# Key transposes at three due times, and block 0's second mixing, low-rank store and weight sums at other quarters, in an attention and FFN kernel

## The reference

```python
h = einsum('bct,bcd->bdt', x, W[condition])          # mixes the 64 rows of a batch
q, k, v = h @ Wq.T, h @ Wk.T, h @ Wv.T               # 32 heads, 8 key/value heads, 128 wide
q, k = rmsnorm(q), rmsnorm(k)
x = x + softmax(q k^T / sqrt(128) + alibi) v @ Wo.T
x = x + FFN(low_rank_adapted_linear(x))              # FFN weights: base plus a Fourier update
```

## Time and profile before

| | |
|---|---|
| median of 3 runs | 2388.41 us (2387.01 to 2389.78) |
| the profiled execution | 2391.09 us, of which 2389.2 us is the span from the first to the last instruction |
| TensorE busy | 2349.9 us of the span, 98% |
| VectorE, ScalarE, GpSimd busy | 1775.3, 1468.2, 284.6 us |
| TensorE clock | full, but for one stretch of about 13 us near 153 us, and the last microseconds |
| DMA | 316.16 MB, 132 GB/s over the span |

### The profile page before, as it was taken

The page is one execution under the profiler, slowest core; times in us unless marked ns, Lnnn a source line. Parts: engine busy times, 40 slices in busy tenths (PEclk is TensorE's granted clock), DMA queues, the critical chain, the costliest instruction groups (busy, mean ns, idle before and its releaser), DMA issues.

```text
span 2389.2 us, 33429 instructions
## 1 busy us (share of the span) xinstructions
PE 2349.9 (98%) x11706; PEld 1964.7 (82%) x11706; DVE 1775.3 (74%) x2930; ACT 1468.2 (61%) x3625; POOL 284.6 (12%) x336
## 2 busy tenths in 40 slices
PE   8989999999999999999999999999999999999998
PEld 6878888888888888888888888888888888888886
DVE  6768868696847878787846777777866686969691
ACT  4246667576625857576824857576844676767660
POOL 1222010101011001010021101010121101010111
PEclk9989999999999999999999999999999999999999
DMA  6765434442542242424443242423254242424250
GB/s 256 261 240 209 156 133 151 148 138 69 196 147 88 86 143 73 144 76 133 138 155 115 71 159 71 159 71 124 93 174 141 81 150 71 147 83 137 69 201 35
DMA packets 88440, 316.16 MB, mean 132 GB/s; under 512 B 12716, under 2 KB 13228, under 8 KB 87124
## 3 DMA queue, kind: packets, MB, share of 16 engines
q1 hardware_dynamic: 70292, 247.14, 31.3%
q0 software_dynamic: 16256, 62.92, 7.3%
q10 hardware_dynamic: 1728, 3.98, 0.5%
HBM read 282.54 MB, written 31.46 MB: 131 GB/s over the span
## 4 chain that ended last, share of the span: by engine, by line
PE 86%; DVE 8%; DMA 2%; issue 2%; ACT 1%; POOL 0%; ACTq 0%; DVEq 0%; POOLq 0%
PE main L1027 73%; PE qt_bank L1188 3%; PE s_bank L1204 3%; DVE ring L1497 2%; PE s_bank L1205 2%; PE pv_bank L1225 1%; PE pv_bank L1224 1%; PE pt_bank L1212 1%; PE pt_bank L1027 1%; DVE values L1628 1%; DVE lefts L1497 1%; DMA sums<-in_wo 1%; DVE quads L1715 1%; DMA acc<-in_x 1%; DVE qn L1642 1%
## 5 line engine op out<-in xcount | busy, mean ns | idle before, releaser
L1027 PE MATMUL main<-ring,act_hi 128*128 128x512 f32 x3584 | 1149.4, 402 | 1.1 <-DVE ring L1497 0.6
L1027 PEld LDWEIGHTS main<-ring,act_hi 128*128 128x128 f32 x3584 | 642.6, 189 | 114.8 <-issue 3.0
L1027 PE MATMUL main<-ring,act_lo 128*128 128x512 f32 x1792 | 702.7, 392 | 0.0
L1027 PE MATMUL main<-ring,lefts 128*128 128x512 f32 x2688 | 626.2, 392 | 0.0
L1497 DVE TENSOR_TENSOR ring<-raw,ring 128x1024 fp32r<-128x1024 f32 x448 | 548.3, 1229 | 51.0 <-ACT ring L1235 49.4
L1027 PEld LDWEIGHTS main<-ring,lefts 128*128 128x128 f32 x2688 | 500.2, 188 | 101.3
L1235 ACT ACTIVATE ring<-raw 128x1024 fp32r<-128x1024 f32 x448 | 472.3, 1057 | 174.7 <-PE main L1027 158.2
L1027 PEld LDWEIGHTS main<-ring,act_lo 128*128 128x128 f32 x1792 | 337.4, 188 | 74.5
L1836 POOL TENSOR_TENSOR rstd<-mean,half 128x4 f32<-128x4 f32 (+1 forms) x192 | 173.8, 905 | 1559.9 <-DVE mean L1622 1555.0
L1368 ACT ACTIVATE sq<-main 128x128 f32<-128x128 f32 x640 | 168.6, 276 | 78.1 <-PE main L1027 72.9
L1396 ACT ACTIVATE prob<-score,peak 128x64 f32<-128x64 f32 x512 | 136.1, 336 | 97.0 <-DVE peak L1680 96.3
(11 more groups left out here) (168 smaller groups left out, 2571.8 us busy)
## 6 DMA issues: line engine op xcount, KB each, us to landing
raw<-in_wq SPq DMA_DIRECT2D x128, 512.0 KB, 4.3
raw<-t_scratch SPq DMA_DIRECT2D x128, 512.0 KB, 3.3
raw<-in_wo SPq DMA_DIRECT2D x96, 512.0 KB, 3.3
raw<-in_wkv SPq DMA_DIRECT2D x64, 512.0 KB, 4.0
sums<-in_wo POOLq DMA_DIRECT2D x32, 512.0 KB, 8.0
t_scratch<-sums POOLq DMA_DIRECT2D x32, 512.0 KB, 4.1
raw<-f_scratch SPq DMA_DIRECT2D x32, 512.0 KB, 5.2
acc<-in_x POOLq DMA_DIRECT2D x16, 512.0 KB, 4.2
```

The source lines that it names most:

```text
L1027: mm = eng.matmul(bank, a, b, start=start and n == 0 and m == 0, stop=stop and n == len(terms) - 1 and m == 2, skip_group_check=further)
```

## The change

The due times of `key_t`, `k_hi` and `k_lo` are no longer one for all: for kv0 of blocks 1 to 3, the first three steps have 2.8, 3.4, 3.9 ("mixing"); the last step of kv1, kv2 and kv3 of each block has 4.8, 5.4, 5.9 ("projection": the `o` unit follows it); all others keep 3.8, 4.4, 4.9 ("queries"). In block 0 the mixing of tiles 2 and 3 goes from quarters 5 and 9 to 2 and 6, `fx_store` from quarter 4 to 14, the t1 to t4 and stores of the first round in `blocks()` by 3.5 quarters later (its loads stay), and the next two rounds, loads and all, by 1.5 quarters later.

```diff
-          tq=2.8, tq_hi=3.4, tq_lo=3.9, tk=3.8, tk_hi=4.4, tk_lo=4.9,
+          tq=2.8, tq_hi=3.4, tq_lo=3.9,
...
+KEYS_AT = dict(mixing=(2.8, 3.4, 3.9), queries=(3.8, 4.4, 4.9), projection=(4.8, 5.4, 5.9))
...
+FIRST_MIX = 2, 2
...
-ROUND_AT = (0.5, 17, 33.5, 104, 180)
+ROUND_AT = (0.5, 18.5, 35, 104, 180)
...
-        self.at(0, 4, lambda: self.add("fx_store"))
+        self.at(0, 14, lambda: self.add("fx_store"))
...
+            wait = 3.5 if start < QUARTERS else 0
             for i, stage in enumerate(("t1", "t2", "t3", "t4")):
-                self.at(start, 7.2 + 1.5 * i, lambda pair=pair, c=c, stage=stage: self.sums_add(pair, c, [stage]))
-            self.at(start, 12.8, lambda pair=pair, c=c: self.sums_store(pair, c))
+                self.at(start, wait + 7.2 + 1.5 * i, lambda pair=pair, c=c, stage=stage: self.sums_add(pair, c, [stage]))
+            self.at(start, wait + 12.8, lambda pair=pair, c=c: self.sums_store(pair, c))
...
-            if k in (1, 2):
-                self.later(1, lambda k=k: self.mix(0, k + 1))
+            if k in (0, 1):
+                self.later(FIRST_MIX[k], lambda k=k: self.mix(0, k + 2))
...
+        (kind, blk, n), i = self.units[self.steps[k][0]], self.steps[k][1]
+        if n == 0:
+            place = "mixing" if blk > 0 and i < TILES - 1 else "queries"
+        else:
+            place = "projection" if i == TILES - 1 else "queries"
+        transposed, upper, lower = KEYS_AT[place]
...
-            self.at(base, AT["tk"], transpose)
+            self.at(base, transposed, transpose)
...
-            self.at(base, AT["tk_hi"], lambda: self.add("k_hi", k))
-            self.at(base, AT["tk_lo"], lambda: self.add("k_lo", k))
+            self.at(base, upper, lambda: self.add("k_hi", k))
+            self.at(base, lower, lambda: self.add("k_lo", k))
```

## The result

The changed kernel takes 2373.85 us in the median of 5 runs (2372.03 to 2375.95), the kernel before 2387.01 beside it (5 runs, 2384.35 to 2389.78): ratio 0.9943, 95% interval 0.9932 to 0.9953, 13.2 us or 0.55% faster. The forecast was 2367.0 with 2362 to 2377 as its range: the direction and the range held, and of the 21.5 us expected only about 13 came. The time lies outside the 2362 to 2371 of the forecast's own case, in the 2372 to 2377 of rival B. The profiled execution took 2375.95 us (span 2374.0), 15.1 less than the 2391.09 of before. Lines of the kernel are 14 higher now: L1041 is the main matmul, L1202 the transposes, L1125 and L1127 the mixing, L1656 the scale, L1663 the gain.

What follows compares the result with a forecast made beforehand. TensorE, busy 98% of the span, bounds the kernel by its work plus its holes. Gains of 11.5 (projection), 0.9 (mixing) and 9.1 (block 0) sum to 21.5 us: 2388.41 less that is 2366.9, forecast 2367, range 2362 to 2377.

Steps and rivals of the forecast that it cites:

- the forecast's own case: Whole kernel: all three gains come, 21.5 us together, for 2362 to 2371 us; chance 0.74.
- rival B: Block 0: POOL gives the start back, late store landings delaying loads and the first query's `rstd`; 2372 to 2377, chance 0.15.
- Projection, 12 x 0.96 = 11.5 us: Last step of kv1 to kv3: key transposes a quarter later no longer wait for `gain`, 0.96 us each, twelve times.
- Rivals C and E: `o` unit: C, projection waits only move, 2378.5, chance 0.05; E, `k_hi` makes ring halves late, 2394, chance 0.03.
- Block 0, 9.1 us: Start of block 0: 10.5 us gained by the second key transpose, less 0.9 and 0.5 given back.
- I take 0.5: Block 0, first queries: POOL's `rstd` blocked by the second round's loads, between 0 and 5.5 us, taken as 0.5.
- The loss at the start: Block 0, first quarter to second key transpose: 32.47 us holding 20.06 us of work at full clock, so 12.4 lost.
- The sums of rounds 2 and 3 ... taken as 0: Block 0: these sums each move one place on, with the same DVE work, +/-1 us, taken as 0.
- Mixing, 0.9 us: Block transitions: `k_lo` empties `qt_bank` sooner for the last mixing, 0.43 us back at two of three transitions.

Runs made afterwards that it cites:

- e4: The changed kernel with `fx_store` at quarter 8 in place of 14: 2376.64 us, ratio 0.9961 to the kernel before.
- e6: The changed kernel with the second round's four loads 2.9 quarters later, behind the first query's `rstd`: 2371.62 us, ratio 0.9932; a second time 2370.59 us, 0.9924.
- e8: The changed kernel with the second round's loads behind the first query's `rstd` and all keys at the places of before: 2384.78 us, ratio 0.9982.

## Why the prediction was right, and where it was not

- **Projection, 12 x 0.96 = 11.5 us: right.** The stretches gave 11.3, the kernel with this part alone 11.3 in its medians (9.8 by its ratio, 6.7 to 13.1 by its interval). Rivals C and E are out: no wait moved into the `o` units. The kernel with block 0 mended shows the other side, the twelve waits of 8.8 us with the keys where they were.
- **Block 0, 9.1 us: wrong, it was 0.** The step that failed is "I take 0.5, ... since before the change the last load came 6.2 us after the stores' issue ... and the same distance here gives a load at about 173.5". It came at 177.67, 9.6 us after the stores' issue ended: the last store took 9.8 us to land in place of 6.4. The same distance could not be carried over, since other transfers now run beside the stores. Without `fx_store` beside them the last store took 8.4 us in place of 9.8 (e4). That the DMA engines no longer stand idle ahead of the stores is not it either: in the kernel with the store at 8 they moved 0 GB/s from 161 to 166 us, and the stores took up to 8.4. What all nine profiles with the changed block 0 share is the raw-weight load issued 0.9 us behind the first t store and the next 2.3 us later; in the three with the old one, the first comes 5.0 to 5.3 us behind it. This sorts the profiles, last store 8.4 to 11.1 us against 6.4, but no run moves the raw loads alone, so it is argued and not shown. The hole and the clock behind it cost 6.8 us in B, and 5.9 in the block-0 kernel. I had written down the rival with this mechanism and gave it 0.15; its cause, `fx_store`, explains less than half of the lateness (e4), its queue the right one (e6). That the range held is this rival's doing: the sum itself was 6.9 us off.
- **The loss at the start was overrated.** 12.4 us were read from one profile. With the same code in block 0, A was 1.8 and 3.9 us shorter in two others; against the mean of the three (42.2) A gained 7.3, where the profiled pair shows 9.05. The chain of steps in A was right to 0.6 us; what it was subtracted from was an execution with an unusually large loss.
- **"The sums of rounds 2 and 3 ... taken as 0": 1.2 us** in C, in all four kernels. The two profiles show where: a score wait of 0.66 at 232.6 that before had not, and 0.79 in place of 0.57 and 0.67 at two query transposes.
- **Mixing, 0.9 us: the size per case was right, the sum can't be measured.** Each case is a transition at which TensorE waits for `k_lo`. From the start of `x_hi` to the mixing it is 725.91 - 722.75 = 3.16 us before, and 2.71 in the changed kernel, ScalarE's and TensorE's timelines at block 2's transition:

```profile
1272.33 1.06 ACT L1249 ACTIVATE x_odd<-acc 128x1024 fp32r<-128x1024 f32 x1 [3.34 <-DMA acc<-in_x]
...
1275.04 0.39 PE L1125 MATMUL qt_bank<-mixw,x_odd 128*128 128x256 f32 x1 [0.66 <-DVE k_t L1511]
```

  0.45 us, forecast 0.43. The other profiles agree: the distance is 3.15 us at each of the five such waits in kernels with the old places (before, projection alone, e8) and 2.7 us at each of the eight in kernels with the new ones. But how large the hole is, and at how many of the three transitions there is one (none to two), differs between executions: in the changed kernel run again the same hole is 1.76, and the transition 52.15 us against 49.95. The 2.6 us by which the profiled pair differs here are mostly chance: in the projection and block-0 kernels, with the key places of before, all six transitions had 48.5 to 49.9 us too. By the runs the part is 0.9996 [0.9987, 1.0005], which can't be told from nothing.
- **Together:** by the experiments 11.3 + 0 + some 0.9 = 12.2, measured 13.2 (11.2 to 16.2 by the interval) and, the second time, 9.9 (7.4 to 13.9). The best version is the changed kernel with the four loads behind the `rstd`: 16.5 and 19.2 us faster than before in the medians of its two measurements.

## What to carry to other kernels

Where an engine's queue holds both computations and DMA issues that wait for landings, note for each such issue when it leaves the queue and when the next computation behind it is wanted: that margin (here 4.6 us) is what an earlier start uses up if the landings don't come earlier with it, as here, where the stores were issued 4.3 us earlier and the last load left at the same time. A hole with a half-clock stretch behind it should be read from several executions before its length is booked as a gain. And a transpose that waits each time for the same operation is cheap to cure: any place behind that operation, if its bank has no next user nearby.

## What the hardware did that I had not expected

- **Half clock after short holes, and none after longer ones.** Holes of 3.8 to 4.1 us were followed by 3.4 us at half clock (mixing alone, block 0 alone, changed kernel again, projection two quarters later), 6.8 (changed kernel), two times 3.4 (projection alone, with a second hole of 1.85 us between) and 13.7 (before, with a second one of 2.44). But a hole of 1.76 us at 1273.69 in the changed kernel run again was followed by 3.4 us too, and so were 1.94 at 199.42 (later rounds), 1.91 at 719.96 (projection two quarters later) and 1.80 at 719.19 (block 0 mended). The 2.62 and 1.76 us in the kernel with the store at 8, the 3.06 in the one with later rounds, and another 1.8 at 183.3 in the kernel with block 0 mended were not. Stretches of the changed kernel run again, at 1273:

```profile
1273.00:1276.00 3.00, 1.24 (x9) 0.78 (x7) 2.12 (x4) 2.34 (x8) 0.34 (x1) 1.00 0.00 0
1276.30:1279.70 3.40, 3.40 (x15) 3.11 (x15) 3.23 (x10) 1.39 (x4) 0.05 (x1) 0.51 0.00 0
```

  So the length of a hole alone does not decide it; what does is left open. It makes a hole of 1.8 us cost 1.8 at one place and 3.5 at another (1.8 and half of 3.4).
- **One and the same 512 KB store took 3.0 to 11.1 us to land**, and a 2048 KB store 6.3 us at quarter 14, 10.3 at 8 and 13.3 at 4: it was quickest where the loads of the first round had landed before it was issued.
- **GpSimd did not let the ready `rstd` past the waiting loads**, 5.3 us long. The Trainium skill (TensorE: Matmul & The Clock Gate, section Architectural detail) says the queues of ScalarE, VectorE and GpSimd are strictly in order, and this trace agrees.
